# Attention block over 16 images: the last low part of the weights runs ahead of the next image's sums, and the last output is added and stored another way

## What is computed

```python
h = group_norm(x, norm_gamma, norm_beta)
q, k, v = conv1x1(h, wq, bq), conv1x1(h, wk, bk), conv1x1(h, wv, bv)
attn = softmax(einsum('bci,bcj->bij', q, k) * C**-0.5, axis=2)
out = conv1x1(einsum('bcj,bij->bci', v, attn), wo, bo)
return x + out
```

## Time and profile before

| | us |
|---|---|
| Median of 3 runs | 2061.13 (2060.94 to 2061.47) |
| The profiled execution, its own time | 2061.74 |
| Its span in the trace | 2060.0 |
| TensorE busy | 1991.7 (97%) |
| VectorE busy | 1636.6 (79%) |
| ScalarE busy | 999.8 (49%) |
| GpSimd busy | 329.3 (16%) |

### The profile page before, as it was taken

The page is one execution under the profiler, slowest core; times in us unless marked ns, Lnnn a source line. Parts: engine busy times, 40 slices in busy tenths (PEclk is TensorE's granted clock), DMA queues, the critical chain, the costliest instruction groups (busy, mean ns, idle before and its releaser), DMA issues.

```text
span 2060.0 us, 29828 instructions
## 1 busy us (share of the span) xinstructions
PE 1991.7 (97%) x9924; PEld 1694.4 (82%) x9924; DVE 1636.6 (79%) x2287; ACT 999.8 (49%) x1529; POOL 329.3 (16%) x238
## 2 busy tenths in 40 slices
PE   7999999999999999999999999999999999999998
PEld 6888878888787887878878788887888878788787
DVE  7897786978879688696887879778697886968856
ACT  6464453645436464454644536445364543646443
POOL 2012120111202022020121202212011120202202
PEclk9999999999999999999999999999999999999999
DMA  6435252362424534154351533525235242353302
GB/s 235 148 143 154 75 150 92 143 163 116 98 92 150 155 143 108 55 173 132 143 148 34 179 106 143 153 70 154 92 143 163 102 112 92 147 158 143 77 36 41
DMA packets 55467, 255.45 MB, mean 124 GB/s; under 512 B 8208, under 2 KB 8208, under 8 KB 50832
## 3 DMA queue, kind: packets, MB, share of 16 engines
q1 hardware_dynamic: 34896, 221.53, 28.1%
q0 software_dynamic: 18432, 33.56, 10.8%
q10 hardware_dynamic: 2112, 0.01, 0.1%
HBM read 214.18 MB, written 74.45 MB: 140 GB/s over the span
## 4 chain that ended last, share of the span: by engine, by line
PE 70%; DVE 10%; ACT 8%; issue 7%; DVEq 0%; ACTq 0%; POOL 0%; POOLq 0%
PE psum L381 24%; PE psum L382 23%; PE psum L383 23%; DVE h_lo L904 3%; ACT big_hi L708 2%; DVE big_lo L1082 2%; ACT room L599 2%; DVE big_lo L1098 2%; ACT scores L698 2%; ACT h_hi L608 2%; DVE scores L1075 1%; DVE scores L889 1%; DVE room L1089 1%; DVE red L1070 0%; DVE mean_scaled L880 0%
## 5 line engine op out<-in xcount | busy, mean ns | idle before, releaser
L381 PE MATMUL psum<-big_hi 128*128 128x512 f32 x1056 | 421.5, 399 | 53.6 <-DVE big_lo L1082 50.5
L382 PE MATMUL psum<-big_lo,big_hi 128*128 128x512 f32 x1056 | 419.2, 397 | 0.0
L383 PE MATMUL psum<-big_hi,big_lo 128*128 128x512 f32 x1056 | 418.9, 397 | 0.0
L381 PE MATMUL psum<-big_hi,h_hi 128*128 128x512 f32 x896 | 348.7, 389 | 0.0
L382 PE MATMUL psum<-big_lo,h_hi 128*128 128x512 f32 x896 | 348.6, 389 | 0.0
L383 PE MATMUL psum<-big_hi,h_lo 128*128 128x512 f32 x896 | 348.5, 389 | 0.0
L381 PEld LDWEIGHTS psum<-big_hi 128*128 128x128 f32 x1056 | 203.3, 192 | 102.7 <-DVE big_lo L1082 56.9
L1061 DVE TENSOR_TENSOR scores<-psum,room 128x512 f32<-128x512 f32 x192 | 130.7, 689 | 195.7 <-ACT room L764 145.7
L381 PE MATMUL psum<-w_split,h_hi 128*128 128x256 f32 x896 | 253.6, 283 | 0.1
L382 PE MATMUL psum<-w_split,h_hi 128*128 128x256 f32 x896 | 253.6, 283 | 0.0
L383 PE MATMUL psum<-w_split,h_lo 128*128 128x256 f32 x896 | 253.6, 283 | 0.0
(11 more groups left out here) (126 smaller groups left out, 3453.9 us busy)
## 6 DMA issues: line engine op xcount, KB each, us to landing
w_split<-kept_t SPq DMA_DIRECT2D x15, 3584.0 KB, 11.8
w_split<-kept_v SPq DMA_DIRECT2D x15, 3584.0 KB, 11.3
room<-in_x SPq DMA_DIRECT2D x64, 512.0 KB, 3.4
out<-scores POOLq DMA_DIRECT2D x128, 256.0 KB, 6.1
room<-in_x SPq DMA_DIRECT2D x60, 256.0 KB, 5.5
red<-in_x SPq DMA_DIRECT2D x30, 256.0 KB, 3.1
wide<-in_x SPq DMA_DIRECT2D x30, 256.0 KB, 4.3
kept_t<-w_split SPq DMA_DIRECT2D x1, 3584.0 KB, 11.0
```

The source lines that it names most:

```text
L381: nc.tensor.matmul(o, a_hi, b_hi, start=start, stop=False, skip_group_check=True)
L382: nc.tensor.matmul(o, a_hi, b_lo, start=False, stop=False, skip_group_check=True)
L383: return nc.tensor.matmul(o, a_lo, b_hi, start=False, stop=stop, skip_group_check=True)
```

## The change

Two things, which do not touch each other.

First, on VectorE, the eighth low part `low_p(b, 1, 7)` moves from behind the second of the next image's four sums to right behind the seventh low part; the four sums then stand together.

```diff
-                for n in range(4, NJ - 1):
+                for n in range(4, NJ):
                     low_p(b, 1, n)
                 if more:
                     for n in range(3):
                         low_h(b + 1, n)
...
-                    sum_h(b + 1, 0)
-                    sum_h(b + 1, 1)
-                low_p(b, 1, NJ - 1)
-                if more:
-                    sum_h(b + 1, 2)
-                    sum_h(b + 1, 3)
+                    for n in range(4):
+                        sum_h(b + 1, n)
                 add_up(b, 1)
```

```diff
+        rest = room[:, 7, :]
...
+                else:
+                    sp.wait_ge(h_split, count(b, 7, 7))
+                    sp.dma_start(rest, x_d[b][:, KC - 1, HALF:N]).then_inc(rest_held, 16)
+                    sp.wait_ge(rest_in, count(b, 16, 16))
+                    sp.wait_ge(last_added, 1)
+                    sp.dma_start(out_d[b, KC - 1, :, HALF:N], scaled(2 * KC - 1)).then_inc(last_stored, 16)
...
             for n in range(2 * KC):
-                sp.wait_ge(out_stored[n], 16 * B)
+                sp.wait_ge(out_stored[n], 16 * (B if n < 2 * KC - 1 else B - 1))
+            sp.wait_ge(last_stored, 16)
...
-                for n in range(2 * KC):
+                for n in range(2 * KC if more else 2 * KC - 1):
...
                 if not more:
-                    for n in range(KC, 2 * KC):
+                    for n in range(KC, 2 * KC - 1):
                         bias_output(b, n)
...
+                if not more:
+                    dve.wait_ge(o_scaled, count(b, 8, 4 * KC))
+                    dve.wait_ge(rest_held, 16)
+                    nc.vector.scalar_tensor_tensor(scaled(2 * KC - 1), scaled(2 * KC - 1), out_bias[:, KC - 1:KC], rest,
+                                                   ALU.add, ALU.add).then_inc(last_added, 1)
```

More of the change, by code:

```diff
@@ L239, in attention_program @@
         turn_step, o_scaled, o_done = sem("turn_step"), sem("o_scaled"), sem("o_done")
+        rest_held, last_added, last_stored = sem("rest_held"), sem("last_added"), sem("last_stored")
         block = ctx.enter_context(nc.Block())
```

## The result

The changed kernel takes 2028.64 us (median of 4 runs, 2027.66 to 2031.75) against 2061.03 us before: a ratio of 0.9846 with a 95% interval of 0.9829 to 0.9863, 32 us faster. The prediction said 2006.0 us with a range of 1995 to 2028: the direction was right, the size was not, and the time lies 0.6 us outside the range. The profiled execution took 2027.78 us with a span of 2025.8, 34.2 us less than the span before.

What follows compares the result with a forecast made beforehand. TensorE, busy 97% of the span, was taken as the bound. Passages net of new stalls gain 54.2 us, the last output 0.9, together 55.1: from 2061.74 to 2006.6, adjusted to the median 2006.0 us, range 1995 to 2028.

Steps and rivals of the forecast that it cites:

- The stall that goes: TensorE's wait for the eighth low part and the low clock behind it: 5.23 us at 13 passages, 3.52 at two.
- Product 2: In the next image's make_t, waits for ScalarE's copy a: met by 0.2 us only, no stall.
- Product 6: In make_t, waits for copy b behind the bias additions of outputs 4 and 5: new stall of 0.89 us.
- Product 1 of r = 0: In make_t, waits for sum D3, held by landings of outputs 0 to 3: mean stall 0.50 us, ends 0 and 1.3.
- Product 1 of r = 1: In make_t, waits for D3 behind landings of outputs 4 to 7: hidden by 1.5 us, nothing taken, bounds 0 and 1.
- Rival 2: Landings come later, outputs 4 to 7 meeting SyncE's four loads: either D3 1 us later per passage, 2021 us; chance 11%.
- The clock: Rival: clock falls behind the two new small stalls; 2032 us if at every passage, 2019 at half; chance 10%.
- The last output: At the program's end, VectorE's addition and a plain store: 0.9 us gained, bounds 1.4 gained and 0.8 lost.
- The 0.4 us that the prediction set beside its own figure: Gain at the program's end by the skill's first-byte times alone, about 0.6 us from SyncE against 1 from GpSimd.

Runs made afterwards that it cites:

- e3: Changed kernel, but SyncE issues the next image's four loads only when output 7 has landed: 2003.36 us, ratio 0.9726.
- e4: Changed kernel, but the wait for landings of outputs 4 to 7 moves from D3 of r = 1 to the sums that overwrite their tiles: 2003.52 us.
- e2: Kernel before with the new way of the last output alone, low parts in the old order: 2059.14 us, ratio 0.9989.
- e6: Changed kernel, but ScalarE makes the copy b ahead of the bias additions of outputs 4 and 5: 2037.25 us, ratio 0.9884.
- e5: Changed kernel, but the r = 0 sums D3, D1, D2 and B11 wait for one landing each, not all four ahead of D3: 2028.51 us.
- e7: Changed kernel with the edits of e4, e5 and e6 together: 1988.24 us, ratio 0.9645.
- e8: Changed kernel with the edits of e4 and e5, outputs 4 to 7 scaled ahead of two low parts of h, copies a and b in free rows: 1986.04 us.

## Why the prediction was right and wrong

**The stall that goes: right.** 5.23 us a passage (3.52 us of idling and 1.71 us of low clock) was the price, and all of it went, at all 15 passages: the outputs take 43.55 us in every image that another one follows. Nothing else took its place there.

**Product 2: nearly.** The 0.2 us of slack were used up: the matmul behind this place comes 0.11 us late at nearly every passage, with no idle time to speak of ahead of it.

**Product 6: right.** 0.89 us predicted, 0.75 us measured in most passages, and 0.11 us for the slow matmul behind it.

**Product 1 of r = 0: right in kind, half in size.** 0.50 us taken; the stall is between 0 and 0.9 us, 0.25 in the mean.

**Product 1 of r = 1: this is the step that failed.** The prediction took nothing, with bounds of 0 and 1 us. Measured over the 14 passages that have it: 0.74 to 2.06 us, 1.34 in the mean. The working carried the delay from the bias of output 6 to D3, 9.23 us in the trace before, over to the new place unchanged, and got a slack of 1.5 us. The bias of output 6 did come where it was expected, 6.18 us behind TensorE's start of `make_t` (the prediction has 925.9 - 919.73 = 6.17). The delay from it to D3 is what failed: 11.8 to 12.9 us at these 14 passages, 12.0 in the mean. The 9.23 us had in them a landing of 7.0 us at a time when transfers 4 and 5 had 2.6 us of lead over 6 and 7, and when three of the four loads had landed before output 7 was issued (at 928.9, 930.1 and 931.3, against 931.7). Now all four transfers are issued back to back within 3.5 us, together with the loads, none of which has landed when output 7 is issued, and the last transfer lands 9.4 to 10.6 us after its issue. Of the two differences the loads are the one that counts: in e3 the four transfers are as close together, without the loads, and land after 6.3 to 7.2 us. D3 is some 2.8 us later in the mean, which eats the slack of 1.5 and gives a stall of the size measured. Behind it come two things that the working did not have: the low parts behind D3 reach the scores 0.22 us late, and 0.11 us are lost at the first matmul of each. e3 and e4 price all of this at 25 us, which is the gap of 22.6 us between the forecast of 2006.0 and the measured 2028.64, and 2.5 us more; of these the end of the program gave 1 to 2 us.

The trace before held a warning that the prediction passed by. At the two passages where the clock had kept its level, TensorE came to `make_t` 1.7 us sooner, and there output 7 landed after 8.5 and 7.5 us, against 5.6 to 7.7 us at the other 13. This is the first of the two, output 7 of the fourth image (issued at 553.2):

```profile
DMA to landing us min/median/max: 8.5/8.5/8.5
```

In e2's trace it is the same: 8.9, 8.7 and 7.7 us at the three passages that kept the clock, 5.8 to 7.2 at the others. The delay to D3, too, was longest at these two passages of the trace before, 10.8 and 9.8 us. The 9.23 us were read at a passage where TensorE came later, and at the two the lead of transfers 4 and 5 was the same 2.6 us; what they had more of was loads in flight.

Rival 2 named this mechanism and priced it at 1 us a passage, 2021 us; it was given 11% and stands closest to what happened. The range took it in only at that price, and ended 0.6 us short. The range covered this case through the rival alone; the sum had the term at nothing.

**The slow first matmul: missed.** It shows in the kernel before at the two passages that kept the clock (0.50 us for the first matmul there), but the working did not count it. Some five places at 0.11 us are 0.5 us a passage; this is about the size by which the stalls at product 6 and at product 1 of r = 0 were taken too long (0.4 us), so the two errors cancel, by luck.

**The clock: right in the profiled execution.** There it did not fall behind the new stalls. The four executions took 2027.66, 2027.78, 2029.51 and 2031.75 us at a mean granted clock of 1.000, 0.999, 0.998 and 0.997, so it may have fallen a few times in the slower ones; that is worth 4 us at the most, and no trace shows where. e6 shows a limit near: there the waits for the copy and D3 sum up to 36.8 us in place of 27.7, and it fell at two of 15 passages. In e5 they sum up to 31.7, and it fell at none, not even behind the longest:

```profile
1052.24 0.50 PE L393 MATMUL psum<-h_hi,w_split 128*128 128x512 f32 x1 [2.64 <-DVE scores L986]
```

**The last output: right in sign, low in size.** 0.9 us predicted, 1.9 measured (interval 0.4 to 4.3), 2.8 by the traces. The store lands after 2.1 us and not 3.1, and the span ends 0.4 us behind it, where it had ended 1.2 us behind the landing of the adding transfer; the working kept the 1.2 us as they were. The 0.4 us that the prediction set beside its own figure is at the very edge of the interval, and the landing alone is 1.9 us shorter.

**The sum by the traces.** The stage of `make_t` takes 22.0 us in the middle passage where 19.04 are work, so with what is lost ahead of the scores and behind them some 3.1 us are given back of 5.0 us in the mean (75.0 / 15). Between the start of the first image's scores and that of the last `make_t` this leaves 75.0 - 14 x 3.1 = 31.6 us gained, and the traces show 31.6 (1869.8 against 1838.1 us). The last `make_t` takes 2.1 us more, for its stalls at product 6 and at product 1 of r = 0, and the end 2.8 us less. That makes 32.3 us, the difference of the medians (32.4).

The spans of the two profiled executions differ by 34.2. The other 1.8 us lie ahead of the first image's scores, which begin at 60.5 in place of 62.3, and they are the clock's: in the kernel before it was 0.53 from 39.20 on the earlier trace rows, and in the changed kernel's profile the same stretch reads:

```profile
39.20:42.70 3.50, 3.50 (x16) 2.88 (x16) 3.50 (x4) 2.48 (x6) 0.00 (x0) 1.00 1.13 442
```

The change does not touch this place. The clock fell here in six of the ten profiles (before, e2, e3, e6, e7 and e8) and not in the other four. Two spans compared by themselves would have put 1.8 us down to the change that are not its own.

## What to carry to other kernels

When a stall on the bounding engine goes, everything that did not move with it is the new deadline: list what comes at a fixed time (the other engines' chains, and above all the landings of transfers), and price each transfer at its new neighbours, not at the delay it had among the old ones. Where several stalls stand ahead of one fixed time, they do not add up, and taking away the first ones alone gives nothing or a loss (e5, e6), while with the last one gone they are worth their full price (e7). A trace can hold a sample of the new state: here the two passages at which TensorE came sooner already had the slower landings. A wait for a transfer should stand at the instruction that overwrites its tile and not at the head of the group; here that alone was worth 25 us (e4).

## What the runs showed of the hardware

Four adding transfers of 256 KB from GpSimd, issued within 3.5 us: the last lands 6.3 to 7.3 us after its issue when the four plain loads of 256 KB from SyncE do not run beside them (e3, and the last passage of the changed kernel), and 9.4 to 10.6 us when they do (the changed kernel; up to 10.8 in e4). A single plain store of 256 KB from SyncE at the end landed after 2.1 us, where a single adding transfer from GpSimd took 4.0; how much of this is the adding and how much the other queue, no run tells.

Behind a stall of `make_t` at the full clock, the first two matmuls start 0.30 to 0.34 us apart instead of 0.23, some 0.11 us more, down to the shortest stalls read (0.13 us of lost time, in e8).

In the kernel before, the clock fell behind 13 of 15 stalls of 3.4 us (12 of 15 in e2). It fell behind none of the stalls of the passages in the profiles of the changed kernel and of e5, which reach 2.1 and 2.8 us of lost time, and in e6 behind two of 15, at 2.0 and 2.7 us, while 2.2 and 2.3 us kept it. So in these traces the length of a stall alone does not say whether the clock falls.
